# The first four heads' scores in fp32 from unstacked keys and masked queries, a down projection by column groups, and W1's sums in pieces

## The reference, cut to what matters

```python
# adapter, with the expert of each sequence
hidden = gelu(x @ down_W.T + down_b)                      # 256 -> 64
hidden = hidden @ Wsel.T + bsel + emb                     # 64 -> 64, expert by domain id
x = layernorm(hidden @ up_W.T + up_b + x) * gamma + beta
# block, modulated by the timestep
x = layernorm(x) * (1 + scale) + shift
q, k, v = (x @ W + b for W, b in ((Wq, bq), (Wk, bk), (Wv, bv)))   # 16 heads of 16
scores = q @ k.T / 4 + attention_bias                     # bias: 8 x 16 x 512 x 512
ctx = softmax(where(src_mask, -inf, scores)) @ v
x = x + ctx @ Wo + bo
h = layernorm(x) * g2 + beta2
out = x + gelu2(h @ W1 + b1) @ W2 + b2                    # gelu2(z) = z * sigmoid(1.702 z)
```

## Time and profile before

| | us |
|---|---|
| median of 3 runs | 922.28 |
| lowest, highest | 920.33, 923.88 |
| the profiled execution | 922.32 |
| its span in the profile | 920.5 |
| PE busy in it | 890.1 |
| DVE, ACT, POOL busy | 700.4, 717.1, 708.8 |

### The profile page before, as it was taken

One profiled execution on the slowest core, in us unless ns is written; L12 is line 12 of the kernel. 1 busy time (PEld: TensorE's weight loads), 2 busy tenths in 40 slices (PEclk: granted clock), 3 DMA queues, 4 the chain that ended last, 5 costly groups with the idle time before them and its releaser, 6 DMA issues.

```text
span 920.5 us, 20973 instructions
## 1 busy us (share of the span) xinstructions
PE 890.1 (97%) x6566; PEld 672.1 (73%) x6566; DVE 700.4 (76%) x1893; ACT 717.1 (78%) x1703; POOL 708.8 (77%) x425
## 2 busy tenths in 40 slices
PE   8888989999999999999999999999999999999988
PEld 5666657777777777777777777777777777677766
DVE  6688688787787878788787877877787887675652
ACT  8688789788887879878797878879697787867651
POOL 3889968787888867897787878879687977886700
PEclk9999999999999999999999999999999999999999
DMA  7799788768977699766978679776997669765400
GB/s 248 232 312 320 242 246 270 233 206 234 287 218 222 203 255 295 221 217 206 264 242 241 214 228 291 222 209 213 261 263 221 201 199 286 222 198 176 125 2 23
DMA packets 147039, 206.36 MB, mean 224 GB/s; under 512 B 14249, under 2 KB 61674, under 8 KB 146930
## 3 DMA queue, kind: packets, MB, share of 16 engines
q1 hardware_dynamic: 145538, 203.71, 73.7%
q10 hardware_dynamic: 1392, 1.31, 0.5%
HBM read 183.98 MB, written 20.99 MB: 223 GB/s over the span
## 4 chain that ended last, share of the span: by engine, by line
PE 81%; POOL 6%; issue 4%; DVE 3%; ACT 3%; DMA 2%; SPq 1%; DVEq 0%; POOLq 0%; ACTq 0%
PE tp L1054 20%; PE pv L1006 11%; PE sc L1045 11%; PE la L968 11%; PE lc L953 10%; PE lb L730 5%; POOL bias_s L568 5%; PE lb L987 3%; PE lb L746 2%; DMA bias_s<-in_bias 1%; DVE xm L1391 1%; PE la L712 1%; ACT bias_s L1282 1%; PE lc L704 1%; DMA mask_raw<-in_mask 1%
## 5 line engine op out<-in xcount | busy, mean ns | idle before, releaser
L568 POOL TENSOR_TENSOR bias_s<-mask_f,bias_s 128x1024 f32<-128x1024 f32 x248 | 582.3, 2371 | 109.7 <-DMA bias_s<-in_bias 109.1
L1720 DVE CUSTOM_DVE_ANT_0 bias_s<-sc,bias_s 128x512 f32<-128x512 f32 x512 | 347.5, 683 | 161.5 <-PE sc L1045 152.1
L1282 ACT ACTIVATE bias_s<-bias_s,mx 128x512 f32<-128x512 f32 x512 | 371.3, 726 | 70.2 <-DVE mx L1720 67.9
L1054 PE MATMUL tp<-ident,bias_s 128*128 128x128 f32 x2048 | 309.1, 274 | 6.5 <-DVE pT L1727 2.2
L1054 PEld LDWEIGHTS tp<-ident,bias_s 128*128 128x128 f32 x2048 | 251.9, 141 | 85.8 <-issue 16.4
L1288 ACT COPY pT<-tp 128x512 f32<-128x512 f32 x335 | 195.2, 583 | 96.5 <-PE tp L1054 94.2
L1045 PE MATMUL sc<-stk,stq 128*128 128x512 bf16 x512 | 195.2, 381 | 4.8 <-DVE mx L1720 3.6
L968 PE MATMUL la<-w_s,act_s 128*128 128x256 f32 x496 | 124.3, 380 | 0.0
L1006 PE MATMUL pv<-pT,v_all 128*32 128x256 f32 x2048 | 123.8, 382 | 0.0
L1727 DVE COPY pT<-tp 128x512 f32<-128x512 f32 x177 | 121.0, 684 | 1.9 <-PE tp L1054 1.8
L953 PE MATMUL lc<-hT,w_s 128*128 128x256 f32 x464 | 119.4, 380 | 2.5 <-ACT hT L1231 1.9
(11 more groups left out here) (242 smaller groups left out, 867.0 us busy)
## 6 DMA issues: line engine op xcount, KB each, us to landing
bias_s<-in_bias SPq DMA_DIRECT2D x256, 512.0 KB, 4.8
stq<-q_parts SPq DMA_DIRECT2D x126, 96.0 KB, 4.1
stk<-k_parts SPq DMA_DIRECT2D x124, 96.0 KB, 3.9
k_parts<-kb SPq DMA_DIRECT2D x32, 192.0 KB, 2.3
q_parts<-qb SPq DMA_DIRECT2D x31, 192.0 KB, 2.4
k_parts<-kb SPq DMA_DIRECT2D x32, 128.0 KB, 2.3
stq<-q_parts SPq DMA_DIRECT2D x63, 64.0 KB, 4.8
stk<-k_parts SPq DMA_DIRECT2D x62, 64.0 KB, 4.1
```

What stands on the lines that cost most here:

```text
L568: pool.tensor_tensor(tile, mask_f[:, :, :], tile, ALU.subtract).then_inc(s["masked"], 1)
L1054: last = pe.transpose(tp[n % 2][:, kt * P:(kt + 1) * P], bias_s[:, n // 2 % NB, n % 2, kt * P:(kt + 1) * P], ident[:, :])
L1282: act.activation(tile, tile, ACT.Exp, bias=mx[:, t:t + 1], scale=-1.0, accum_out=sums[:, j, head_of(hh):head_of(hh) + 1]).then_inc(s["prob ...
L1720: dve.tensor_tensor_reduce(out=tile, in0=sc[t % 2][:, :], in1=tile, scale=1.0, scalar=BIG, op0=ALU.add, op1=ALU.min, accum_out=mx[:, t:t + ...
```

## The change

It does five things.

1. Group 0 of chunk 0 has no stacks. ACT and DVE copy k of the first eight heads in fp32 to `k_first` (the tile `ctxn`), one sequence half each. DVE copies q four times, multiplied by a column `of_head` that is 1 on the head's 16 partitions and 0 elsewhere (`pick_head`, into a part of `pT[1]`). One fp32 matmul over all 128 partitions then gives the head's score (8 matmuls of 128 x 512). The selection matrices, `stack`, `move_stack` and the memsets for them are gone.
2. The bf16 parts of the first half are still needed, by group 2 and by chunk 1. They are now made in slots 1.3 to 7.6 of iteration 0 (`first_part` on ACT, `first_rest` and `first_low` on DVE) from fp32 copies in SBUF. SP stores them behind the loads of heads 8 and 9, and loads group 0's keys for chunk 1 at slot 19.6.
3. The down projection is eight matmuls of 32 columns over 256, on four column groups, at slot 21.6 right behind `weigh`. Two of the groups hold the second 256 rows, so gelu is two instructions over 256 columns; the bias has a copy on partitions 64 to 127.
4. W1's sums stand in six pieces at slots 8, 9, 10 and 15, 15.6, 16.6; the scalings move to 18.6 and 20.3, the first lift to 21. In iteration 1 POOL takes the inverse roots two heads earlier.
5. The experts' weights are turned into `lc` instead of `pv`, and the first fold moves from slot 13.3 to 15, its copy from 15.6 to 17.

```diff
-PE_AT = dict(up=0.3, v=(1.0, 2.0), q=(8.6, 10.0), xt1=13.0, k=(15.6, 16.3), down=(24.3, 25.3),
+PE_AT = dict(up=0.3, v=(1.0, 2.0), q=(8.6, 10.0), xt1=13.0, k=(15.6, 16.3), down=21.6,
-EXPERTS_AT = dict(turn=9.6, spread=11.6, fold=(13.3, 20.0, 25.0), copy=(15.6, 22.3, 27.3))
+FIRST_AT = dict(k_hi=3.6, rest=(1.3, 5.0), mid=(2.3, 6.6), low=(3.3, 7.6))
+EXPERTS_AT = dict(turn=9.6, spread=11.6, fold=(15.0, 20.0, 25.0), copy=(17.0, 22.3, 27.3))
-W1_AT = dict(sums=(9.0, 15.0), scale=(16.0, 19.6), lift=(20.3, 22.0))
+W1_AT = dict(sums=(8.0, 9.0, 10.0, 15.0, 15.6, 16.6), scale=(18.6, 20.3), lift=(21.0, 22.0))
...
+        k_first = ctxn[:, :, :].rearrange("p c t -> p (c t)")
+        q_first = rin
+        q_picked = pt1[:, 0:GH * CH].rearrange("p (h t) -> p h t", h=GH)
+        k_rest = hT
...
-            store_early_keys(0, 0)
-            store_early_keys(1, 0)
-            sp.wait_ge(s["half_lo"], 3)
-            sp.dma_start(q_d[0, 0].rearrange("n p t -> p n t"), qb[:, :, 0:CH]).then_inc(q0_out, 16)
             store_early_keys(0, 1)
...
             load("b2_in", [(b2_r[:, :], b2.to_broadcast([P, D]))])
+            sp.wait_ge(s["half_lo"], 1)
+            sp.dma_start(q_d[0, 0].rearrange("n p t -> p n t"), qb[:, :, 0:CH]).then_inc(q0_out, 16)
+            store_early_keys(0, 0)
+            store_early_keys(1, 0)
+            load_queries(0, 2)
             load_keys(0, 2)
-            load_queries(0, 2)
...
-                    if i == 0 and t == 13.0:
-                        sp.wait_ge(s["sc_ready"], 4)
+                    if i == 0 and t == 19.6:
+                        load_keys(0, 0)
...
-                last = pe.matmul(lc[:, :], down_w[:, ct, :], (xT_second if b == 1 else xT)[:, ct, :], start=(ct == 0), stop=(ct == CT - 1))
+                src = (xT_second if b == 1 else xT)[:, ct, :]
+                for n in range(4):
+                    last = pe.matmul(lc[32 * n:32 * n + 32, 0:CH], down_w[:, ct, 32 * (n % 2):32 * (n % 2) + 32],
+                                     src[:, CH * (n // 2):CH * (n // 2 + 1)], start=(ct == 0), stop=(ct == CT - 1),
+                                     tile_position=(0, 32 * n))
...
-                        pe.wait_ge(s["half_lo"], 1)
+                        pe.wait_ge(s["k0_first"], 1)
...
+                    if i == 0 and t < TG:
+                        pe.wait_ge(s["k0_first"], 1)
+                        pe.wait_ge(s["k1_first"], 1)
+                        pe.wait_ge(s["q0_picked"], hh + 1)
+                        pe.matmul(sc[t % 2][:, :], q_picked[:, hh, j * P:(j + 1) * P], k_first,
+                                  start=True, stop=True).then_inc(s["sc_ready"], 1)
+                        return
...
-                act.activation(h2[0:A, :], lc[0:A, :], ACT.Gelu, bias=vec[0:A, VEC["down_b"]:VEC["down_b"] + 1]
+                act.activation(h2[0:A, 0:CH], lc[0:A, 0:CH], ACT.Gelu, bias=vec[0:A, VEC["down_b"]:VEC["down_b"] + 1])
+                act.activation(h2[0:A, CH:2 * CH], lc[A:2 * A, 0:CH], ACT.Gelu, bias=down_b2[A:2 * A, 0:1]
...
+            def first_part(u, part):
+                if part == 0 and u == 2:
+                    act.wait_ge(s["k1_first"], 1)
+                if part == 1:
+                    act.wait_ge(s["half_rest"], u)
+                if u == 1:
+                    ins = act.copy(qb[:, part, 0:CH], q_first[:, :])
+                else:
+                    src = k_rest if part else k_first.rearrange("p (c t) -> p c t", c=2)
+                    for c in range(2):
+                        ins = act.copy(kb[c][:, part, 0:CH], src[:, c, :])
+                ins.then_inc(s["half_mid" if part else "half_hi"], 1)
...
+            def pick_head(h):
+                dve.tensor_scalar(q_picked[:, h, :], early_bank("q0", 0)[:, 0:CH], nbq[:, 0:1], of_head[:, h:h + 1],
+                                  ALU.add, ALU.mult).then_inc(s["q0_picked"], 1)
...
+            def first_rest(u):
+                dve.wait_ge(s["half_hi"], u)
+                if u == 1:
+                    ins = dve.tensor_tensor(q_first[:, :], q_first[:, :], qb[:, 0, 0:CH], ALU.subtract)
                 else:
+                    for c in range(2):
+                        ins = dve.tensor_tensor(k_rest[:, c, :], k_first[:, c * CH:(c + 1) * CH], kb[c][:, 0, 0:CH],
+                                                ALU.subtract)
+                ins.then_inc(s["half_rest"], 1)
...
+            dve.wait_ge(s["half_p"], 2)
+            dve.tensor_scalar(k_first[:, CH:2 * CH], early_bank("k1", 0)[:, 0:CH], vec[:, VEC["bk"]:VEC["bk"] + 1],
+                              None, ALU.add).then_inc(s["k1_first"], 1)
+            dve.wait_ge(s["half_p"], 3)
+            dve.wait_ge(s["of_head"], 1)
+            pick_head(0)
+            pick_head(1)
+            early_rest("k0")
+            pick_head(2)
+            early_rest("q0")
+            pick_head(3)
+            early_low("k0")
+            early_rest("k1")
+            early_low("q0")
```

266 lines of the change are left out of this document (98 added, 168 removed).

## The result

| | kernel before | changed kernel |
|---|---|---|
| median | 922.35 us (920.33 to 926.19, 14 runs) | 926.71 us (921.73 to 930.26, 14 runs) |
| profiled execution | 922.32 us, span 920.5 | 927.36 us, span 925.6 |

The ratio is 1.0041, with a 95% interval of 1.0027 to 1.0055: 4 us slower, where 6.7 us faster had been forecast. 926.71 lies outside the range.

A forecast was written before the change was run, and what follows sets the result against it. PE was taken to bound the kernel (busy 97% of the span), with order and latency binding the first two chunks; 922.3 - 4.2 - 2.5 - 0 = 915.6 us, range 909.5 to 920.8.

The forecast's parts named there:

- Part 1: Down projection in chunks 1, 3, 5, 7, 9 and 11: 0.7 us saved each, 4.2 us in all, bounds 3.5 and 5.2.
- Part 2: W1's sums in pieces, chunk 1: gain of 2.5 us, between 0 and 4.2.
- the 1.28 with most of its clock loss: Chunk 1: gain nearest to removing PE's 1.28 us wait and most of the 1.7 us lost to slow clock.
- the scaling comes later: Chunk 1: with sums in pieces, ACT's scaling moves later; no cost was given for it.
- The last rival: Chunk 1's order gives nothing and down projections leave waits behind them: 918.8 us, chance 0.05.
- Part 3: First four heads in fp32, chunk 0: net 0, between a gain of 2.3 us and a loss of 3.
- So PE is about 1.5 us ahead at slot 14: Chunk 0: PE gains a lead of about 1.5 us by slot 14, which late biases then eat.
- It goes out near 56.5: SP's queue, chunk 0: head 10's bias is issued near 56.5 us instead of 52.34, behind four stores and nine loads.
- Part of the lag is absorbed in a wait that SP had: SP's queue after head 12's bias, some 3 us late: an existing wait takes up part of that lag.
- Six loads, 2.8 us: SP's queue before slot 19.6's key store: six new loads of group 0's keys cost 2.8 us.
- the second rival: Loads bind in chunk 0: head 10's 4.2 us lag passes on, half clock follows at its end; 921.3 us, chance 0.16.
- The collision of DVE and POOL: Chunk 0's six new DVE subtractions each wait about 1.2 us for POOL's masking; 919.2 us if half do, chance 0.05.

The follow-up runs named there:

- down_216: Kernel before with only the column-group down projection, all of it at slot 21.6 behind the weighing: 919.89 us, ratio 0.9971.
- w1_order: Kernel before with column-group projection, W1's sums in pieces, scalings at slots 17.3 and 19.3, first lift at 20.3: 919.61 us, ratio 0.9959.
- w1_only: Kernel before with only W1's sums in pieces, new scaling and lift slots and chunk 1's earlier inverse roots: 923.58 us, ratio 1.0009.
- down_w1: Kernel before with the column-group projection at slot 21.6 and W1's sums in pieces: 919.41 us, ratio 0.9967.
- bias_first: Changed kernel with heads 10 and 11's biases issued before the low-part waits, chunk 0's later biases one place earlier: 923.43 us, 1.0017 of kernel before.
- low_later: Changed kernel with the subtraction for the queries' lowest part two slots later: 925.63 us, ratio 1.0034 to the kernel before.
- keys_later: Changed kernel with the six new key loads at slot 24.3 instead of 19.6, behind later biases: 926.25 us, ratio 1.0040 to the kernel before.
- w1_early: Changed kernel with W1 (1 MB) loaded right behind b2 instead of at slot 14: 930.04 us, ratio 1.0075 to the kernel before.
- bias_keys: bias_first with the six key loads at slot 22.3 and the queries' lowest part two slots later: 928.66 us, ratio 1.0071 to the kernel before.
- heads_only: Kernel before with only the fp32 treatment of the first four heads, with moved key load and fold: 928.28 us, ratio 1.0064.
- down_only: Kernel before with only the column-group down projection, at slot 24.3: 920.56 us, ratio 0.9979.
- heads_down_bias: bias_keys with W1's sums, scalings and lifts as in the kernel before: 929.51 us, ratio 1.0072 to the kernel before.

## Why the prediction was wrong

**Part 1 was right, term by term.** It said 0.7 us a batch, bounds 0.59 and 0.86; the five later ones gave 0.86, the upper bound: PE waited nowhere for ACT's second gelu. The sixth, in chunk 1, gave nothing: in the change it waited 0.71 us for the lift, and down_216, which has the projection alone, takes 70.36 us from weighing 4 to 9 against 69.58. 4.3 against 4.2; alone at 21.6 the part measures 3.45 in the total.

**Part 2 failed at what it counted.** The stall shrank and the clock loss went (2.16 us between weighings 4 and 5), and the sum took them as time of the kernel: "the 1.28 with most of its clock loss", 2.5 us. Alone it measured 1.0 us slower, and its interval takes in no change. DVE and ACT set the pace there, so the 1.7 us of slow clock had cost nothing by the first lift (16.34 and 16.35 us behind weighing 4, with and without them), and down_216 lost them without any pieces. The step "the scaling comes later" also priced the scaling at nothing at its new place, two slots before the lift that needs it, where DVE waited 2.33 us for it. But that wasn't what decided: w1_order took the wait away, and the total stayed. The last rival was right in its first half, that the order of chunk 1 gives nothing.

**Part 3 failed at the lead and at the queue.** It came to 0, measured alone 5.7.
- "So PE is about 1.5 us ahead at slot 14": it wasn't. Score 0 came earlier for want of the stacks, but from the last projection of the setup to weighing 0 the changed kernel takes 24.75 us, and w1_only and down_w1, with the old chunk 0, take 24.76 and 24.77 (the kernel before 25.17). That is with the fold and its wait (2.2 us) gone from that stretch: the longer fp32 scores and DVE's work must have taken it (their shares were not split). There was no lead to set against late biases.
- "It goes out near 56.5": head 10's bias went at 60.20. The low parts of k were there at 52.90, not near 50.5, partly because of the 2.94 us subtraction, and the four stores and nine loads took 7.3 us instead of 6, with no wait for a landing in them. bias_first shows what the place of the biases in the queue was worth, 2 to 3 us.
- "Part of the lag is absorbed in a wait that SP had": it was passed on nearly whole. The biases of heads 11, 12, 14 and 15 went out 7.0, 6.4, 6.9 and 9.7 us later than before. The wait that was to absorb it is one for the landing of chunk 1's queries, and their store had moved by the same 6 us.
- "Six loads, 2.8 us": 4.0 in the queue, and head 15's bias was masked from 87.06, not 81. What then followed was the second rival: a wait at the end of chunk 0 (3.11 us) and half clock behind it. It stood at 921.3 with a chance of 0.16, too low by 5.4 us, because it priced the turn of the chunks at 4.7 us where it cost 6.4, gave part 2 1.5, and had nothing for the 1.4 of the second half of chunk 0 and the 0.9 before weighing 0.

The other steps: score 0 came at 36.19. Its maximum ran at 37.95, not 36.6, behind the picks and parts on DVE; the paced slots began at 41.3, not 40.0, and score 8 came at 50.55, not before 49.

**The collision of DVE and POOL is real, and was small.** The rival gave it 1.2 us for each subtraction; one in six met masks fully and lost 2.5, one lost 0.4 (it took 0.82). The Trainium skill, GPSIMD Engine Reference, Specifications, has this rule (POOL's SBUF interface is shared with VectorE, contended by DVE instructions with two SBUF inputs); the trace agrees, 2.94 us against 0.40. low_later shows that it decided nothing: with the subtraction at 0.40 the waits before scores 11 and 12 and the late biases stayed.

**The clock.** Behind the waits of 2.8 to 5.3 us before score 32 (the changed kernel, keys_later, w1_early, bias_keys) the window from 90 to 95 us shows a granted clock of 0.50 to 0.66, part or all of it at the lower level; in bias_first, with 0.90, it is 1.00 from 85 to 100 us. A wait of 1.28 us before score 52 was followed by the lower level in the kernel before and in heads_only, and not in down_216, down_only and heads_down_bias; what decided was not found. In the setup the clock fell at different times in executions of the same code: over 12 to 24 and 24 to 36 us it was 1.00 and 0.86 in the kernel before, and 0.72 and 1.00 in w1_only, which shares that setup, both with the same span of 920.5. So the 0.9 us that the changed kernel was late at weighing 0 is not laid to the change.

**Open.** What of the rest of the heads' loss (some 3 us) is the six loads' own transfer was not measured apart: no run left them out, since the next chunks need the keys. Issuing them from another engine's queue was not tried; the Trainium skill, Trainium Kernel Development and Optimization, Key Constraints, says that this saves the issue time alone. By that rule up to the 4.0 us of queue at 75.05 would go and the transfer would stay; no run here shows it.

## What to carry to other kernels

A part of PE's work that is taken out of a stretch where PE is the chain comes back in full (0.86 us each, five times); in a stretch where another engine or the loads set the pace it comes back as a wait, and so does a clock that no longer falls. Before a stall of one engine is counted as time, look at where the engine that releases it stands against a fixed event in a run that lacks the stall. Where a change moves a store later in an in-order DMA queue, walk the whole queue behind it to the last load that something needs, landing waits included, and don't let a wait further on absorb the lag before checking that its own releaser hasn't moved too.
